# A gated delta-rule attention block on one core: convolution taps that read PSUM, state updates summed by TensorE, narrower state reads

## The reference

```python
q = silu(causal_dwconv(x @ Wq.T))          # 4 taps, depthwise
k = silu(causal_dwconv(x @ Wk.T)) * 128 ** -0.5
v = silu(causal_dwconv(x @ Wv.T))
a, beta = sigmoid(x @ Wa.T + ba), sigmoid(x @ Wb.T + bb)
def step(S, q, k, v, a, beta):             # S is 128 x 128 for each pair
    Sk = S @ k
    S = a[:, None] * S - (beta * (Sk - v))[:, None] * k
    return S, S @ q
```

## Time and profile before

| | |
|---|---|
| median of 3 runs (lowest to highest) | 2976.94 us (2976.73 to 2979.72) |
| the profiled execution, its time | 2981.21 us |
| its span in the trace | 2979.4 us |
| PE busy | 2244.8 us (75%) |
| PE weight loads busy | 1688.4 us (57%) |
| DVE busy | 1992.2 us (67%) |
| ACT busy | 1375.2 us (46%) |
| POOL busy | 818.7 us (27%) |
| mean clock granted to PE | 0.874 |

### The profile page before, as it was taken

The page is one execution under the profiler, slowest core; times in us unless marked ns, Lnnn a source line. Parts: engine busy times, 40 slices in busy tenths (PEclk is TensorE's granted clock), DMA queues, the critical chain, the costliest instruction groups (busy, mean ns, idle before and its releaser), DMA issues.

```text
span 2979.4 us, 67827 instructions
## 1 busy us (share of the span) xinstructions
PE 2244.8 (75%) x24976; PEld 1688.4 (57%) x24976; DVE 1992.2 (67%) x4412; ACT 1375.2 (46%) x3128; POOL 818.7 (27%) x546
## 2 busy tenths in 40 slices
PE   5999778777772776777777677767777776299998
PEld 3455566655552666666666666666666665234443
DVE  5223888889882777777777777777777777613234
ACT  2003667766762344444544453445445444044434
POOL 0000777666667121122212122211222121200000
PEclk9999999999996789888978887898889788599999
DMA  5000444445547243334333332433333333311110
GB/s 213 7 14 36 186 166 168 168 182 203 203 173 268 68 140 131 110 102 133 115 113 117 132 108 92 140 131 113 99 133 115 113 116 115 103 74 70 71 56 21
DMA packets 139512, 359.01 MB, mean 120 GB/s; under 512 B 11312, under 2 KB 92968, under 8 KB 126424
## 3 DMA queue, kind: packets, MB, share of 16 engines
q1 hardware_dynamic: 139176, 354.92, 33.5%
q0 software_dynamic: 48, 0.16, 0.0%
HBM read 226.97 MB, written 128.07 MB: 119 GB/s over the span
## 4 chain that ended last, share of the span: by engine, by line
PE 47%; issue 19%; ACT 12%; DVE 11%; POOL 7%; DMA 3%; SPq 0%; DVEq 0%; ACTq 0%; POOLq 0%
PE PS L1289 9%; ACT arena L678 5%; POOL arena L487 4%; PE PS L1395 4%; PE PS L1422 4%; PE PS L1328 3%; PE PS L1277 3%; ACT arena L683 3%; PE PS L1160 3%; PE PS L1201 3%; DMA arena<-beta_d 3%; PE PS L1303 2%; PE PS L1316 2%; PE PS L1249 2%; PE PS L1217 2%
## 5 line engine op out<-in xcount | busy, mean ns | idle before, releaser
L878 DVE SCALAR_TENSOR_TENSOR arena<-arena,SM 128x256 f32<-128x256 f32 x1152 | 542.0, 551 | 93.6 <-ACT arena L605 93.6
L1187 PE MATMUL PS<-arena 128*128 x2048 | 492.6, 398 | 145.3 <-ACT arena L605 131.3
L1187 PEld LDWEIGHTS PS<-arena 128*128 128x128 f32 x2048 | 390.5, 193 | 247.4 <-ACT arena L605 144.3
L487 POOL TENSOR_TENSOR arena<-arena 128x512 f32<-128x512 f32 x64 | 334.6, 5266 | 458.8 <-ACT arena L619 458.8
L524 POOL TENSOR_TENSOR arena<-arena 128x256 f32<-128x256 f32 x128 | 98.6, 771 | 1266.9 <-DVE arena L976 1266.9
L1289 PE MATMUL PS<-arena 128*128 128x128 f32 x1920 | 312.0, 311 | 113.3 <-ACT arena L683 109.5
L1289 PEld LDWEIGHTS PS<-arena 128*128 128x128 f32 x1920 | 262.4, 212 | 156.8 <-ACT arena L683 151.5
L678 ACT ACTIVATE arena<-arena 128x128 f32<-128x128 f32 x960 | 302.1, 396 | 0.0
L920 DVE TENSOR_TENSOR arena<-arena,PS 128x512 f32<-128x512 f32 x192 | 127.5, 685 | 246.5 <-PE PS L1328 246.4
L658 ACT COPY arena<-PS 128x512 f32<-128x512 f32 x154 | 90.3, 586 | 414.8 <-PE PS L1217 196.6
L605 ACT ACTIVATE arena<-PS,SM 128x256 f32<-128x256 f32 x384 | 238.2, 625 | 0.0
(11 more groups left out here) (138 smaller groups left out, 3989.0 us busy)
## 6 DMA issues: line engine op xcount, KB each, us to landing
arena<-g_d SPq DMA_DIRECT2D x128, 512.0 KB, 4.2
vas_d<-arena SPq DMA_DIRECT2D x24, 2048.0 KB, 11.4
arena<-vas_d SPq DMA_DIRECT2D x128, 384.0 KB, 3.4
kq_d<-arena SPq DMA_DIRECT2D x8, 4096.0 KB, 11.4
arena<-kq_d SPq DMA_DIRECT2D x16, 2048.0 KB, 9.4
arena<-beta_d SPq DMA_DIRECT2D x8, 2048.0 KB, 9.9
kb_d<-arena SPq DMA_DIRECT2D x8, 2048.0 KB, 6.6
arena<-kb_d SPq DMA_DIRECT2D x16, 1024.0 KB, 6.2
```

Source lines behind the costliest of these rows:

```text
L487: tt(kb, KQST[:, pp, NB * s:NB * (s + 1), 0, :], kb, ALU.mult).then_inc(kb_step, 1)
L878: nc.vector.scalar_tensor_tensor(acc, PRE[:, x % 2, h, :, i:i + PT_], CW[:, w, i, hh:hh + 1], acc, ALU.mult, ALU.add).then_inc(tap_add, 1)
L1187: ins = mm(bank(g % 8)[:, cols * k:cols * (k + 1)].rearrange("p (b n) -> p b n", b=B), W4[:, WSLOT[kind], kt, DH * (h0 + k):DH * (h0 + k + ...
```

## The change

Stage 2: the copy to PRE is gone, and the taps read the raw values from the PSUM bank. So a bank is held until DVE's last tap of its head, q/k/v jobs use 6 banks in turn, and the other 2 go to the "a" jobs. These are done after groups 2 to 9, first with Identity and bias into AST, and one Sigmoid over the whole AST at the round's end (4,096 elements) replaces the 16. The guard of AST (a_stored and sf_stored of the round before) moves to the first "a" job.

Stage 3: update(s) handles one slot: the identity times S (512 columns) and 4 products of 32 rows are summed in the bank. The keys are stored negated (evac "kt"), decay reads PSUM and writes S, and state_add is gone. Slots are read from block 1 on; update(s + 2) and decay(s + 2) stand behind the transposes and the copy of slot s. A read takes the columns of its own pair only (64).

```diff
-JOBS = [("qkv"[x * 4 // H], 4 * (x % (H // 4)) + h, 1) for x in range(NQ) for h in range(4)] + [("a", 2 * i, 2) for i in range(H // 2)]
-NJ = len(JOBS)
+NJ = 4 * NQ
+QB = 6
+A_AFTER = [None, None, 0, 1, 2, 3, 4, 5, 6, 7, None, None]
-U_AT = [[], [0, 1], [2], [3, 4], [5], [6], [7], []]
-ADD_AT = [[], [2, 3], [4, 5], [6, 7, 8, 9], [10, 11], [12, 13], [14, 15], []]
-READ_AT = [[], [], [0, 1, 2], [3, 4, 5], [6, 7, 8], [9, 10], [11, 12, 13], [14, 15]]
+READ_AT = [[], [0, 1], [2, 3, 4], [5, 6], [7, 8, 9], [10, 11], [12, 13], [14, 15]]
...
-                sp.wait_ge(job_free, c * NJ + 8 + NJ)
+                sp.wait_ge(a_ready, c + 1)
                 sp.dma_start(vas_d[:, blocks, 1], ASTf.rearrange("v (l x) -> v l x", x=BP)).then_inc(a_stored, 16)
...
-                pool.wait_ge(job_free, c * NJ + 8 + NJ)
+                pool.wait_ge(a_ready, c + 1)
                 pool.wait_ge(sf_stored, c * 16 + 16)
...
+                def last_tap(x, h):
+                    g = 4 * x + h
+                    w, hh = x * 3 // NQ, 4 * (x % (NQ // 3)) + h
                     act.wait_ge(job_full, c * NJ + g + 1)
...
-                        nc.scalar.copy(PRE[:, x % 2, h], raw)
-                        nc.scalar.activation(ACC[:, x % 3, h], raw[:, :, HALO:HALO + PT_], ACT.Identity, bias=CB[:, w, h0:h0 + 1],
-                                             scale=CW[:, w, KC - 1, h0:h0 + 1]).then_inc(job_free, 1)
+                    raw = bank(g % QB, B * (HALO + PT_)).rearrange("p (b n) -> p b n", b=B)
+                    nc.scalar.activation(ACC[:, x % 3, h], raw[:, :, HALO:HALO + PT_], ACT.Identity, bias=CB[:, w, hh:hh + 1],
+                                         scale=CW[:, w, KC - 1, hh:hh + 1]).then_inc(job_acc, 1)
+                def decay_job(i):
+                    act.wait_ge(a_full, c * (H // 2) + i + 1)
+                    if i == 0:
+                        act.wait_ge(a_stored, c * 16 + 16)
+                        act.wait_ge(sf_stored, c * 16 + 16)
+                    for k in range(2):
+                        h = 2 * i + k
+                        ins = nc.scalar.activation(AST[:, 4 * h:4 * h + 4], bank(QB + i % 2)[:, PC * k:PC * (k + 1)].rearrange("v (b l t) -> v b l t", b=B, t=BL),
+                                                   ACT.Identity, bias=BA[:, h:h + 1])
+                    ins.then_inc(a_free, 1)
                 for x in range(NQ):
                     act.wait_ge(silu_done, c * NQ + x + 1)
                     for h in range(4):
-                        job(4 * x + h)
+                        last_tap(x, h)
                     if x > 0:
                         silu(x - 1)
+                    if A_AFTER[x] is not None:
+                        decay_job(A_AFTER[x])
                 silu(NQ - 1)
-                act.wait_ge(a_stored, c * 16 + 16)
-                act.wait_ge(sf_stored, c * 16 + 16)
-                for g in range(A_JOB, NJ):
-                    job(g)
+                act.wait_ge(a_free, c * (H // 2) + 2 + H // 2)
+                nc.scalar.activation(ASTf, ASTf, ACT.Sigmoid).then_inc(a_ready, 1)
...
                 def decay(s):
-                    act.wait_ge(s_updated, n * 16 + s + 1)
+                    act.wait_ge(up_psum, n * 16 + s + 1)
                     for gi in range(4):
                         p = 4 * (g0 + gi) + j
-                        ins = nc.scalar.mul(S[:, p, :], S[:, p, :], EX[c][:, 6, p:p + 1])
+                        ins = nc.scalar.mul(S[:, p, :], bank(4 + s % 2)[:, 128 * gi:128 * (gi + 1)], EX[c][:, 6, p:p + 1])
...
+                    if m == 1 and nxt:
+                        decay(1)
+                    for s in reads:
                         state_copy(s)
+                        if s + 2 < 16:
+                            decay(s + 2)
+                        next_evac()
                         read_copy(s)
...
                     for i in range(TAPS):
                         for h in range(4):
...
-                            nc.vector.scalar_tensor_tensor(acc, PRE[:, x % 2, h, :, i:i + PT_], CW[:, w, i, hh:hh + 1], acc, ALU.mult, ALU.add).then_inc(tap_add, 1)
+                            raw = bank(g % QB, B * (HALO + PT_)).rearrange("p (b n) -> p b n", b=B)
+                            nc.vector.scalar_tensor_tensor(acc, raw[:, :, i:i + PT_], CW[:, w, i, hh:hh + 1], acc,
+                                                           ALU.mult, ALU.add).then_inc(job_free if i == TAPS - 1 else tap_add, 1)
...
-                    tt(dst, dst, bank(4 + s % 2).rearrange("v (g k) -> v g k", g=4), ALU.subtract).then_inc(s_updated, 1)
...
+                for x in range(NQ):
+                    for h in range(4):
+                        g = 4 * x + h
+                        pe.wait_ge(job_free, c * NJ + g + 1)
+                        project(bank(g % QB, B * (HALO + PT_)), x * 3 // NQ, 4 * (x % (NQ // 3)) + h, HALO).then_inc(job_full, 1)
+                    if A_AFTER[x] is not None:
+                        i = A_AFTER[x]
+                        pe.wait_ge(a_free, c * (H // 2) + i + 1)
+                        for k in range(2):
+                            ins = project(bank(QB + i % 2)[:, PC * k:PC * (k + 1)], 3, 2 * i + k, 0)
+                        ins.then_inc(a_full, 1)
...
-                        p0 = 4 * (g0 + gi) + j // 2 * 2
-                        ins = mm(bank(7)[:, 128 * gi:128 * (gi + 1)].rearrange("v (l x) -> v l x", l=NB), STR[:, s % 2, gi, :],
-                                 KQ[d][:, :, p0:p0 + 2].rearrange("k l p e t -> k l (p e t)"), start=True, stop=True)
+                        ins = mm(bank(7)[:, 64 * gi:64 * (gi + 1)].rearrange("v (l x) -> v l x", l=NB), STR[:, s % 2, gi, :],
+                                 KQ[d][:, :, 4 * (g0 + gi) + j].rearrange("k l e t -> k l (e t)"), start=True, stop=True)
...
+                def update(s):
+                    j, g0 = slot_pairs(s)
+                    rows = slice(32 * j, 32 * j + 32)
+                    if s == 0:
                         pe.wait_ge(corr_sub, n * N_SUB + 16)
+                    elif s >= 2:
+                        pe.wait_ge(s_scaled, n * 16 + s - 1)
+                    dst = bank(4 + s % 2).rearrange("v (g k) -> v g k", g=4)
+                    mm(dst, ident[:, :], S.rearrange("v (g j) k -> v j g k", j=4)[:, j, g0:g0 + 4], start=True, stop=False)
                     for gi in range(4):
+                        ins = mm(dst[:, gi], PT32[rows, g0 + gi, :], KBT[rows, g0 + gi, :], start=False, stop=(gi == 3))
                     ins.then_inc(up_psum, 1)
...
-                    for u in U_AT[m] if nxt else []:
-                        if u not in (1, 4):
-                            update(u)
-                    for k, s in enumerate(reads):
+                    if m == 1 and nxt:
+                        update(0)
+                        update(1)
+                    for s in reads:
                         state_transposes(s)
+                        if s + 2 < 16:
+                            update(s + 2)
                         if preps:
                             prep(m, *preps.pop(0))
                         reads_of(s)
```

More of the change, by code:

```diff
@@ L581, in _ @@
             act.wait_ge(beta_stored, 16 * B)
-            for _ in range(8):
-                nc.scalar.nop().then_inc(job_free, 1)
+            for _ in range(2):
+                nc.scalar.nop().then_inc(a_free, 1)
             for _ in range(3):
@@ L588, in _ @@
             with act.Fori(0, NPC) as c:
-                def job(g):
-                    kind, h0, nh = JOBS[g]
+                def last_tap(x, h):
+                    g = 4 * x + h
+                    w, hh = x * 3 // NQ, 4 * (x % (NQ // 3)) + h
                     act.wait_ge(job_full, c * NJ + g + 1)
[L592 to L602, removed]
-                        raw = bk[:, 0:B * (HALO + PT_)].rearrange("p (b n) -> p b n", b=B)
-                        nc.scalar.copy(PRE[:, x % 2, h], raw)
-                        nc.scalar.activation(ACC[:, x % 3, h], raw[:, :, HALO:HALO + PT_], ACT.Identity, bias=CB[:, w, h0:h0 + 1],
-                                             scale=CW[:, w, KC - 1, h0:h0 + 1]).then_inc(job_free, 1)
@@ L657, in evac @@
                     dst = G2[:, 512 * which:512 * (which + 1)]
-                nc.scalar.copy(dst, src).then_inc(pa_done, 1)
+                if what == "kt":
+                    nc.scalar.mul(dst, src, -1.0).then_inc(pa_done, 1)
+                else:
+                    nc.scalar.copy(dst, src).then_inc(pa_done, 1)
             act.wait_ge(kb_in[0], 16)
@@ L719, in next_evac @@
                             evac(what, w, b, a_item(n, x, nxt))
-                    if m == 2:
+                    if m == 1:
                         act.wait_ge(e_in[c], i * 16 + 16)
-                    if reads:
-                        decay(reads[0])
+                        if nxt:
+                            decay(0)
                     if keys:
@@ L866, in _ @@
```

(9 more changed lines are left out.)

66 lines of the change are left out of this document (19 added, 47 removed).

## The result

The changed kernel takes 3243.3 us (median, lowest 3242.7, highest 3247.8); the kernel before, measured beside it, takes 2978.3: a ratio of 1.0891 (95% interval 1.0872 to 1.0909). The forecast was 3028, range 2945 to 3085. "Slower" was right, the size was not: + 265 us, where + 50 was forecast. The profiled execution has a span of 3245.4 us.

A forecast was written before the change was run, and what follows sets the result against it. No engine is busy throughout: DVE and POOL exclude each other in stage 2, and PE's in-order queue waits in stage 3. 2981.2 − 54 + 105 = 3032 us for the profiled execution, 3028 as a median, range 2945 to 3085.

The forecast's parts named there:

- Slower: Whole kernel: the change ends slower than the kernel before, by more than 0.2%; chance 0.71.
- Stage 2: Stage 2: rounds take 74.1 us against 81.3, and the stage gains 54 us in all, with ends 95 and 20.
- The guard: Stage 2: the first "a" job waits for the last round's sf store, + 2.5 us a round (0 to 8).
- what follows the last tap: End of stage 2: POOL's products no longer wait for L487, − 3.7 us.
- Still excluded: Rival, stage 2: POOL and PSUM taps still block each other, so stage 2 gains nothing, 3082 us; chance 0.06.
- Slow PSUM taps: Rival, stage 2: PSUM taps no longer overlap and take 0.478 us each, 3071 us in all; chance 0.06.
- The updates' work: Stage 3: a slot's update takes 1.81 us on PE, + 1.26, so 16 of them add 20.1 us a chunk.
- Waits filled: Stage 3: updates fill PE's waits, 7.3 us in the handling of slots and 1.6 of the 5.0 at "sel".
- The reads: Stage 3: 64-column reads keep their 8 weight loads and save at most 0.1 us a slot, − 0.5 a chunk.
- PE at half clock … should come back sooner: Stage 3, blocks 1 and 2: full clock returns sooner, − 5.9 us a chunk for old work, + 0.9 for new.
- The clock stays low: Rival, stage 3: PE stays at half clock through block 1, + 7 us a chunk, 3133 us; chance 0.06.
- three signs of being wrong: Block 1 keeps its length, a slot's update takes under 1.3 us, or stage 2's rounds take under 70 us.

The follow-up runs named there:

- e2: The kernel before with only the reads narrowed to 64 columns, and the ACT copy that belongs to them: 3148.7 us, ratio 1.0562.
- e1: The changed kernel with the 128-column reads of the kernel before, and the ACT copy that belongs to them: 3091.7 us, ratio 1.0371.
- e3: The change's stage 2 alone, with stage 3 as in the kernel before: 2929.0 us, ratio 0.9824.
- e4: The change's stage 2 with taps from an SBUF copy, one more ACT pass a job, and the old stage 3: 3091.2 us, ratio 1.0369.
- e6: The change's stage 2 and the old stage 3, plus four unread 512-column products in block 1 of a chunk: 2884.9 us, ratio 0.9676.

## Why the prediction was wrong in size

- **Stage 2, right, with two small errors that cancel.** − 50.7 for − 54; rounds 75.0 on average for 74.1; a group with an "a" job 5.37 for 5.35; the round's end 6.5 for 6.8. The guard was dearer (4.5 us of ACT's time for 2.5). By the last tap the change is 43.3 us ahead (it ends at 863.1, before at 906.4), where 50 was forecast; what follows the last tap gave 7.4 where 3.7 was. "Still excluded" and "Slow PSUM taps" are refuted by L485's and L886's rows, and with them the 65 ns a tap estimated from "VectorE: DVE Perf Modes" (the Trainium skill), section "The TRN2 errata": 476 ns against 478.
- **The updates' work, a little low.** Work + 21.7 for + 19.6, and some 1 us more without the halving's error (an estimate); a slot's update takes 2.04 us for 1.81. The identity product is 0.96 for 0.86, the eight products 1.08 for 0.95.
- **Waits filled, nearly right.** Idle − 9.8 for − 6.8. L683 and L678 (now L686 and L681) hold PE in a chunk for 2.9 us (the "kt" waits that I had kept) and not at all.
- **The reads, the failed step.** "a read of 64 columns keeps its 8 weight loads …, so at most 0.1 us a slot is saved: − 0.5". The saving is within that bound, 0.06 us a slot, so 1.0 us a chunk where 0.5 was booked. That the same records, narrower, could cost the clock was in no term and no rival; the effect of the reads on the clock stood at nothing without a reason. e2 prices that alone at + 168 us in the old kernel, e1 at − 152 in the new one.
- **"PE at half clock … should come back sooner": − 5.9 + 0.9**, the term in which it shows: − 5.0 forecast, + 9.1 measured. It holds for the updates with wide reads (e1: extra − 3.8, low 22.3 where 32.8 was, though its chunk is still + 10.7 us) and fails for the change. "The clock stays low" had half clock in block 1 alone, at + 7 a chunk, from the small tiles of before. Block 1 did stay low in five chunks of fifteen, 7.5 us on average. The longest low stretches came in blocks 6 and 7, 12.2 and 10.2 us where 0 and 1.6 were, with 4.0 in block 5 where none was. Block 6 went from 11.4 to 17.0 us; with wide reads (e1) it has 12.8.
- **Block 1** was forecast at 15 or 16 us. It has 15.1 in the ten chunks where its clock is full and 18.6 on average. Blocks 2 and 3 stayed (14.7 to 14.9, 12.9 to 12.2), block 5 went from 9.9 to 14.0 (12.5 in e1, with no low time, so most of that is work), block 7 from 10.4 to 12.4. None of the three signs of being wrong that I had named showed. What failed among the things to be seen were the chunk (109 us forecast), the clock (0.81, forecast above 0.85) and PE's busy time, + 30.7 us a chunk where some 12 were forecast.
- Even without the clock the direction stands: e1 without the narrow reads is 163 us slower than e3, 10.9 us a chunk against the 7.0 forecast. The updates by TensorE cost work that PE, on the path, has no room for.

Open: which property of the narrow reads lowers the clock (fewer columns in a record, or the changed rhythm of records) was not separated. Why some chunks have block 1 at full clock and others not is open too. Nor were updates by TensorE tried with DVE's adds kept in part. Fillers in block 0, where PE waits 6.7 us for DVE before, in the change and in e1, were not tried, since the head_subs read all eight banks there.

## What to carry to other kernels

When an edit makes TensorE's operands narrower, price the clock beside the records: in e2, reads that were each a little shorter went with a chunk 12% longer. Read the granted clock in windows along the path, at the places where the edited instructions stand, before and after, and count a stretch at half clock as a cost that an edit can create. Where PE waits shortly after such a stretch, a few products that nobody reads may pay for themselves; where the clock is full, they cost their full time.

## What the hardware showed that was not expected

- PE at 1.2 GHz while its records leave 0.46 us idle in 13 (1638 to 1651 in the changed kernel), the same block 1 with the same idleness at either clock (15.1 and 24.2 us), and 0.84 → 0.70 of granted clock from the reads' width alone (e2).
- Taps from PSUM at the rate of taps from SBUF: 476 and 478 ns for 256 elements.
- With two SBUF inputs, which engine pays for the blocking differs between kernels: the same POOL product takes up to 33.2 us before and 1.45 in e4, where the taps lose 158 us instead.
- Adding four unread products of 512 columns, some 3.7 us at full clock, to a chunk shortened it by 3.1 us (e6).
